# Soft mixture of experts behind attention: W1 multiplied into the rows ahead of the gather, and the gather done 64 columns wide in plain f32

## The chip, the cores and the metric

The kernel runs on one core of one Trainium2 chip. The metric is the time of one execution on the device, in microseconds. The program is one launch with a layer of causal attention and a layer of soft experts, both with their layer norms, on inputs of 2 sequences of 1024 rows of 256 numbers in float32.

## The reference

Attention has 16 heads of 128 (4 groups of keys and values) with rotary embedding; it is not changed. Then, per sequence, with x_ln the normalised rows (1024 x 256), E = 16 experts with S = 128 slots each and H = 64:

```
x_n      = x_ln / max(|x_ln|, 1e-12) * scale          # per row
mu_n     = mu / max(|mu|, 1e-12)                      # per slot
logits   = x_n @ mu_n                                 # n, e, s
dispatch = softmax(logits, over the 1024 rows)        # per slot
combine  = softmax(logits, over all 2048 slots)       # per row
slot_in  = dispatch.T @ x_ln                          # e, s, 256
h        = gelu(slot_in @ W1 + b1)                    # e, s, 64
slot_out = h @ W2 + b2                                # e, s, 256
out      = combine @ slot_out                         # n, 256
```

followed by the sum with the input and a layer norm.

## The kernel before

Each engine has its own queue, and all five walk one list of items (`plan_experts` writes it out); an item is issued on the engine that owns its kind, and waits by semaphores for what it needs. So the order of the list is the order on each engine, and an engine that waits holds up all that is behind it.

There are 32 experts g to go through (16 for each sequence), four to a unit (u = 0 to 7), and a slot s of the list is one step of the loop over them, j = s mod 4. For each expert: `logits` on TensorE (12 matmuls of 512 columns, L1387) into the psum tensor `ring`, of which there is one; `top` on VectorE takes the maximum (L1695, L1697); `exp` on ScalarE (ACT) writes exps (L1568); `keep` on ACT copies the logits out (L1579), after which `ring` is free for the next logits; `run` on VectorE keeps a running maximum (L1708); `inverse` is the reciprocal of the sum (L1720). `turn` transposes exps on TensorE in two halves of 512 columns (L1397) into `turned`, two banks used in turn. Each half is copied out twice: `turned_hi` on ACT rounds it to fp32r (L1508), `turned_lo` on VectorE takes the rest (L1713).

A pair of experts is gathered in the odd slots: `gather` (L1419) multiplies the rows, split in the same way into `row_parts`, with the turned exps: for each of 8 tiles of rows and each half c of the 256 features three matmuls of 256 columns (high by high, high by low, low by high). `gathered` on VectorE multiplies by the reciprocals of the sums (L1736), which `wide_inverse` (L1407) and `inverse_taken` (L1726) have spread over the partitions. When a unit is complete, `hidden` multiplies by W1 (L1431, plain f32), `gelu` on ACT (L1589), `output` multiplies by W2 (L1441), `slot_hi` and `slot_lo` split the result, and `spread` (L1481, eight tiles in four pairs over the next slots) multiplies with the weights of `combine`. `peaks`, `peak`, `fade`, `faded` and `wide`, in slot j = 3, carry the maximum of a row from unit to unit; `shift` on GpSimd (POOL) subtracts it.

The psum tensor `small` has two banks, filled in turn by gather, hidden and output. `free_small` makes a fill wait for the reader of the fill two before it. The rows are split by `rows_hi` (ACT, L1502) and `rows_lo` (VectorE, L1756) once a sequence, in slot 0 and, at the change of sequence, behind logits(16). W1 of a unit is loaded by SP after the `hidden` of the unit before.

The matmuls on fp32r tiles stand as one record each in the profile; plain f32 matmuls as two, transposes as one.

Of the kernel before, what the change touches and what calls it, by code (L numbers as in the profile page):

```python
# [214 lines left out]
def attend(shared, gamma_d, beta_d, row_scale_d, nc, y_sb, slot_vectors, mu_loaded, mu_d, x_d, wq_d, wk_d, wv_d, wo_d, head_scale_d, cos_d, sin_d, ident_d, hidden_d):  # L215
# [51 lines left out]
    with ExitStack() as ctx:  # L267
# [13 lines left out]
        norms, inv_mu, ffn_scale = (shared[name] for name in ("norms", "inv_mu", "scale"))  # L281
# [438 lines left out]
        def _(dve):  # L720
# [18 lines left out]
            for kind, *which in plan:  # L739
# [4 lines left out]
                if kind == "mu_inv":  # L744
                    dve.wait_ge(done["mu_norms"], 1)
                    step(nc.vector.tensor_scalar(norms[:, :], norms[:, :], L2_EPS, None, ALU.max))
                    settle()
                    nc.vector.reciprocal(inv_mu[:, :], norms[:, :]).then_inc(done[kind], 1)
# [28 lines left out]
                if kind == "row_scale":  # L777

                    dve.wait_ge(done["row_length"], 1)
                    dve.wait_ge(row_consts_loaded, 3 * 16)  # L780
                    step(nc.vector.tensor_scalar(row_std[:, :], row_std[:, :], L2_EPS, None, ALU.max))
                    settle()
                    step(nc.vector.reciprocal(row_factor[:, :], row_std[:, :]))
                    settle()
                    nc.vector.tensor_scalar(row_factor[:, :], row_factor[:, :], ffn_scale[:, 0:1], None, ALU.mult).then_inc(done[kind], 1)
# [182 lines left out]
def plan_experts(sequences, experts, tiles):  # L968
# [46 lines left out]
    def split_rows(b):  # L1015
        put(("rows_hi", b, 0), ("rows_hi", b, 1))
# [27 lines left out]
    put(("mu_hi", 0), ("mu_lo", 0), ("mu_hi", 1), ("mu_lo", 1))  # L1044
    put(("logits", 0), ("top", 0), ("exp", 0), ("keep", 0), ("run", 0), ("inverse", 0))
    split_mu(2)

    for s in range(total + 3):
# [6 lines left out]
        if changed:  # L1055
            put(("hidden", v))
            spread(v - 1, (4, 5))
# [3 lines left out]
        if live:  # L1061
            for half in range(2):
                put(("turn", s, half), ("turned_hi", s, half), ("turned_lo", s, half))
# [8 lines left out]
        if ripe and j == 0:  # L1072
            if not changed:
                put(("hidden", v))
# [7 lines left out]
        if s == 0:  # L1082
            split_rows(0)
        if ahead and not change:
            put(("top", s + 1))
        if s == 0:
            put(("rows_lo", 0, 0), ("rows_lo", 0, 1))
# [17 lines left out]
        if j in (1, 3) and live:  # L1105
            put(("gather", s // 2, 0))
# [3 lines left out]
        if j in (1, 3) and live:  # L1110
            put(("gather", s // 2, 1))
# [28 lines left out]
        split_mu(s + 3)  # L1140
        early(s)
# [7 lines left out]
def soft_experts(nc, y_sb, raw_mu, mu_loaded, gamma_d, beta_d, mu_d, scale_d, w1_d, b1_d, w2_d, b2_d, ident_d, out_d):  # L1149
# [4 lines left out]
    with ExitStack() as keep:  # L1154
        def stay(name, shape, dt=F32):
# [4 lines left out]
                  "norms": stay("norms", [P, E]), "inv_mu": stay("inv_mu", [P, E]), "scale": stay("scale", [P, 1])}  # L1160
# [4 lines left out]
def experts(nc, shared, y_sb, raw_mu, mu_loaded, mu_d, w1_d, b1_d, w2_d, b2_d, out_d):  # L1165
# [23 lines left out]
    SMALL = ("gather", "hidden", "output")  # L1189
    TURNED = ("turn", "turn_unit", "peaks", "wide", "wide_inverse")  # L1190
    small_fills = [item for item in plan if item[0] in SMALL and (item[0] != "gather" or item[2] == 0)]
# [3 lines left out]
    with ExitStack() as ctx:  # L1195
# [11 lines left out]
        ident, gamma, beta, scale, inv_mu = (shared[name] for name in ("ident", "gamma", "beta", "scale", "inv_mu"))  # L1207
        rowsT = shared["xT"]
        rows = shared["rows"]
        row_parts = sb("row_parts", [P, 2, TILES, D], F32R)  # L1210
# [5 lines left out]
        dispatch = sb("dispatch", [P, 2, TILES, 2, S], F32R)  # L1216
        exps = sb("exps", [P, N])
        inverse_wide = sb("inverse_wide", [P, 2, S])
        gathered = sb("gathered", [P, KT, UNIT, S])
# [74 lines left out]
        def _(sp):  # L1294
# [16 lines left out]
            for kind, *which in plan:  # L1311
# [5 lines left out]
                if kind == "hidden" and which[0] + 1 < UNITS:  # L1317
                    sp.wait_ge(done["hidden"], which[0] + 1)
# [12 lines left out]
        def _(pe):  # L1331
# [3 lines left out]
            def free_small(item):  # L1335

                n = small_at[item]
                if n >= 2:
# [3 lines left out]
                    if kind == "hidden":  # L1342
                        pe.wait_ge(done["gelu"], count("gelu", *which))
# [4 lines left out]
            def free_turned(item):  # L1348

                n = turned_at[item]  # L1350
                if n >= 2:
                    kind, *which = turned_fills[n - 2]
                    if kind == "turn":
                        pe.wait_ge(done["turned_lo"], count("turned_lo", *which))
# [11 lines left out]
            for item in plan:  # L1366
# [33 lines left out]
                if kind == "wide_inverse":  # L1400
# [8 lines left out]
                    last.then_inc(done[kind], 1)  # L1409
                if kind == "gather":  # L1410

                    pair, c = which
                    if c == 0:
                        pe.wait_ge(done["turned_lo"], count("turned_lo", 2 * pair + 1, 1))
                        pe.wait_ge(done["rows_lo"], count("rows_lo", 2 * pair // E, 1))
                        free_small(item)
# [5 lines left out]
                    last.then_inc(done[kind], 1)  # L1422
                if kind == "hidden":

                    (v,) = which
                    pe.wait_ge(done["gathered"], 2 * v + 2)
                    pe.wait_ge(w1_loaded, (v + 1) * KT * 16)
                    free_small(item)
                    for k in range(UNIT):
# [497 lines left out]
```

## Time and profile before

| | |
|---|---|
| median of 3 executions | 1257.33 us (1255.71 to 1257.91) |
| span of the profiled execution (first to last instruction) | 1253.6 us |
| the profiled execution's own time | not recorded beside its span |
| median less span | 3.7 us |
| TensorE, matmuls | busy 1182.8 us, 94% |
| VectorE | busy 802.1 us, 64% |
| ScalarE | busy 756.3 us, 60% |
| GpSimd | busy 698.0 us, 56% |
| mean granted TensorE clock | 0.982 of full speed |

The busy times overlap, since the engines run beside each other. PE stands for TensorE's matmuls, PEld for its weight loads, DVE for VectorE. The attention part fills the first 845 us, the experts the rest.

### The profile page before, as it was taken

Reading aid. Unit: us, or ns where it says so; the run is one execution under the profiler, and the core shown is the slowest. Engines: PE = TensorE matmul, PEld = TensorE weight load, DVE = VectorE, ACT = ScalarE, POOL = GpSimd, SP = SyncE. Lnnn points to the kernel's source line nnn. Section 1 sums busy time; section 2 is a strip of 40 time slices with the busy share of each in tenths; the row PEclk is TensorE's granted clock in tenths of the full one; section 3 lists DMA queues with packets and bytes.
Section 4 is the critical chain, followed back from the end, with each engine's and each line's share of the span. In section 5 each row is a group of like instructions: output and inputs, shape, how many; then the busy total and the mean of one; then the engine's idle time right before and its main releaser. Section 6 shows DMA issues by size and latency. Waiting matters only on the chain. (4 is left out here: it accounts for less than half of the span.)

```text
span 1253.6 us, 22955 instructions
## 1 busy us (share of the span) xinstructions
PE 1182.8 (94%) x7968; PEld 1084.0 (86%) x7968; DVE 802.1 (64%) x1836; ACT 756.3 (60%) x1442; POOL 698.0 (56%) x473
## 2 busy tenths in 40 slices
PE   4899999999999999999999999997899999989996
PEld 3799998899989998999899889986799988888986
DVE  5565675565665676567656666675566666776666
ACT  2555665656665567667665666544678757556552
POOL 1767767657756674777855765401357535426430
PEclk9999999999999999999999999997999999999999
DMA  2331211121111211121112211101101101011101
GB/s 96 81 106 43 55 31 42 31 56 43 30 26 47 56 26 31 43 56 30 43 31 48 50 26 26 27 1 26 30 14 31 30 9 26 18 27 43 34 10 34
DMA packets 48769, 47.52 MB, mean 38 GB/s; under 512 B 13065, under 2 KB 43273, under 8 KB 48401
## 3 DMA queue, kind: packets, MB, share of 16 engines
q1 hardware_dynamic: 48368, 45.99, 14.3%
q8 instruction: 66, 1.08, 0.4%
q14 instruction: 47, 0.38, 0.1%
q10 hardware_dynamic: 288, 0.07, 0.0%
HBM read 24.03 MB, written 2.10 MB: 21 GB/s over the span
## 5 line engine op out<-in xcount | busy, mean ns | idle before, releaser
L527 PE MATMUL ring<-kT,qT 128*128 128x384 f32 (+5 forms) x1152 | 246.6, 350 | 11.9 <-ACT exps L694 6.4
L829 DVE CUSTOM_DVE_ANT_0 ring<-ring,hidden 128x128 f32<-128x128 f32 (+7 forms) x256 | 190.5, 773 | 91.3 <-PE ring L527 91.0
L694 ACT ACTIVATE exps<-ring,neg_max 128x128 f32<-128x128 f32 (+7 forms) x256 | 189.4, 742 | 68.7 <-DVE neg_max L829 68.6
L527 PEld LDWEIGHTS ring<-kT,qT 128*128 128x128 f32 x1152 | 187.0, 190 | 24.8 <-issue 5.2
L710 ACT ACTIVATE exp_parts<-turned 128x512 fp32r<-128x512 f32 x192 | 114.3, 596 | 139.1 <-PE turned L542 116.5
L565 PE MATMUL mix<-exp_parts,v_parts 128*128 128x256 f32 x1152 | 184.5, 296 | 0.4 <-DVE exp_parts L848 0.4
L542 PE MATMUL turned<-ident,exps 128*128 128x128 f32 x1152 | 179.0, 273 | 1.5 <-DVE exp_parts L848 1.0
L848 DVE TENSOR_TENSOR exp_parts<-turned,exp_parts 128x512 fp32r<-128x512 f32 x192 | 131.8, 686 | 48.2 <-ACT exp_parts L710 47.9
L542 PEld LDWEIGHTS turned<-ident,exps 128*128 128x128 f32 x1152 | 141.8, 141 | 20.0 <-ACT exps L694 1.9
L565 PEld LDWEIGHTS mix<-exp_parts,v_parts 128*128 128x128 f32 x1152 | 149.4, 190 | 0.6 <-DVE exp_parts L848 0.6
L954 POOL TENSOR_TENSOR cos_part<-taken,cos_sb 128x1024 f32<-128x1024 f32 x38 | 91.1, 2396 | 100.5 <-ACT taken L662 100.5
L957 POOL TENSOR_TENSOR rotated<-rotated,sin_sb 128x1024 f32<-128x1024 f32 x38 | 91.1, 2397 | 77.1 <-DMA rotated<-taken 77.1
L835 DVE TENSOR_TENSOR mixed<-mix,mixed 128x256 fp32r<-128x256 f32 x128 | 53.6, 418 | 95.8 <-ACT mixed L717 95.8
L1387 PE MATMUL ffn_ring<-xT,ffn_mu 128*128 128x512 f32 x384 | 106.1, 429 | 2.9 <-POOL ffn_mu L1852 2.5
L577 PE MATMUL ring<-wo_sb,mixed 128*128 128x256 f32 x768 | 105.8, 286 | 1.2 <-DVE mixed L835 0.9
L863 DVE SCALAR_TENSOR_TENSOR y_sb<-ring,inv_sum,y_sb 128x256 f32<-128x256 f32 x256 | 105.7, 475 | 0.5 <-PE ring L577 0.3
L561 PE MATMUL mix<-exps_turned,v_sb 128*128 128x256 f32 (+1 forms) x512 | 105.4, 329 | 0.0
L1419 PE MATMUL ffn_small<-ffn_dispatch,ffn_row_parts 128*128 128x256 f32 x768 | 98.5, 285 | 0.3
L577 PEld LDWEIGHTS ring<-wo_sb,mixed 128*128 128x128 f32 x768 | 96.2, 190 | 2.1 <-DVE mixed L835 1.5
L1419 PEld LDWEIGHTS ffn_small<-ffn_dispatch,ffn_row_parts 128*128 128x128 f32 x768 | 94.1, 189 | 1.0 <-DVE ffn_dispatch L1713 1.0
L1387 PEld LDWEIGHTS ffn_ring<-xT,ffn_mu 128*128 128x128 f32 x384 | 76.0, 205 | 21.5 <-POOL ffn_mu L1852 2.7
L961 POOL TENSOR_TENSOR cos_part<-cos_part,rotated 128x1024 f32<-128x1024 f32 x38 | 91.0, 2396 | 5.5
(205 smaller groups left out, 2112.2 us busy)
## 6 DMA issues: line engine op xcount, KB each, us to landing
rotated<-taken SPq DMA_DIRECT2D x76, 256.0 KB, 3.7
raw_q<-in_L_attn_Wq_dram SPq DMA_DIRECT2D x32, 128.0 KB, 3.6
raw_o<-in_L_attn_Wo_dram SPq DMA_DIRECT2D x32, 128.0 KB, 3.3
ffn_mu_next<-in_L_ffn_mu_dram SPq DMA_DIRECT2D x28, 128.0 KB, 2.5
y_sb<-in_L_attn_x_dram SPq DMA_DIRECT2D x2, 1024.0 KB, 7.5
exps_and_mu<-in_L_ffn_mu_dram SPq DMA_DIRECT2D x1, 2048.0 KB, 9.4
ffn_w_sb<-in_L_ffn_W_dram SPq DMA_DIRECT2D x16, 128.0 KB, 2.4
ffn_w_sb<-in_L_ffn_W_dram SPq DMA_DIRECT2D x8, 256.0 KB
```

Of the source, the lines that this page charges most:

```text
L527: last = nc.tensor.matmul(ring_cols(item, half * BANK, piece), qT[:, H % QUERIES, a, i * P:(i + 1) * P], kT[:, G % 2, m, half * piece:(hal ...
L542: last = nc.tensor.transpose(bank[:, k * P:(k + 1) * P], exps[w][:, i, j * P:(j + 1) * P], ident[:, :])
L561: last = nc.tensor.matmul(out, v_sb[:, G % 2, j * P:(j + 1) * P], exps_turned[:, slot_at[H, w, p] % 2, cols], start=j == 0, stop=alone)
L565: last = nc.tensor.matmul(out, v_parts[:, G % 2, a, j * P:(j + 1) * P], exp_parts[:, slot_at[H, w, p] % HELD, m, cols], start=j == 0 and k ...
L577: last = nc.tensor.matmul(ring_cols(item, t * D, D), mixed[:, window % 2, a, t * P:(t + 1) * P], wo_sb[:, H % 2, m, :], start=k == 0, stop ...
L694: nc.scalar.activation(dst, tile, ACT.Exp, bias=neg_max[:, H % 2, i:i + 1], scale=-1.0, accum_out=row_sum[:, H % 2, i:i + 1]).then_inc(don ...
L710: nc.scalar.activation(exp_parts[:, slot % HELD, 0, :], turned[:, n % 2, :], ACT.Copy).then_inc(done[kind], 1)
L829: nc.vector.tensor_tensor_reduce(tile, tile, later, -1.0, 3.0e38, ALU.add, ALU.min, neg_max[:, H % 2, i:i + 1]).then_inc(done[kind], 1)
L848: nc.vector.tensor_tensor(exp_parts[:, slot % HELD, 1, :], turned[:, n % 2, :], exp_parts[:, slot % HELD, 0, :].bitcast(F32), ALU.subtract ...
L863: last = nc.vector.scalar_tensor_tensor(y_row, ring_cols(("output", H, w), t * D, D), inv_sum[:, H % 2, i:i + 1], y_row, ALU.mult, ALU.add)
L1387: last = nc.tensor.matmul(ring[:, half * BANK:(half + 1) * BANK], mu[:, g % 3, a, c, :], rowsT[:, m, c, half * BANK:(half + 1) * BANK], st ...
L1419: last = nc.tensor.matmul(small_at_item(("gather", pair, 0))[:, c * 2 * S:(c + 1) * 2 * S], row_parts[:, a, t, c * P:(c + 1) * P], dispatc ...
```

## The change

W1 is multiplied into the rows first: `fold` computes rows @ W1 for the four experts of a unit, a matrix of 1024 x 256 in eight tiles, two tiles a fill, and the gather then works on its 64 columns per expert instead of on 256 features. `fold` takes the unit rows already in `rowsT` (split in high and low), times W1 split by `w1_hi` (ACT) and `w1_lo` (POOL); `folded_a` (ACT) and `folded_b` (VectorE) copy the fills out in turn and multiply them by the length of each row (`lengths`), with which the division by the length is taken back. The sign of `scale` is kept with the rows and its size goes into `inv_mu`. The gather is in plain f32; the first expert of the pair goes to output partitions 0 to 63, the second to 64 to 127. `row_parts`, `rows_hi`, `rows_lo`, `hidden` and the low part of `dispatch` are gone, and each half of a turn is copied once, the first by ACT (`turned_a`), the second by VectorE (`turned_b`).

The order of the list:

```diff
+    def take_fold(u, i):
+        put(("folded_b" if i % 2 else "folded_a", u, i))
+
+    def fold(u, fills):
+        if u < units and u % 4:
+            for i in fills:
+                put(("fold", u, i))
+                take_fold(u, i)
+
+    def begin(g):
+        u = g // 4
+        put(("logits", g), *[("fold", u, i) for i in range(4)], ("top", g))
+        take_fold(u, 0)
+        put(("exp", g), ("keep", g), ("run", g), ("inverse", g))
+        for i in range(1, 4):
+            take_fold(u, i)
...
-    put(("logits", 0), ("top", 0), ("exp", 0), ("keep", 0), ("run", 0), ("inverse", 0))
+    begin(0)
...
-            put(("gather", s // 2, 0))
+            put(("gather", s // 2))
         if j == 3 and live:
             put(("wide", u, 0), ("widened_a", u), ("wide", u, 1), ("widened_b", u))
...
-        if j in (1, 3) and live:
-            put(("gather", s // 2, 1))
...
         if ahead and not change:
             put(("run", s + 1), ("inverse", s + 1))
         if j in (1, 3) and live:
             put(("gathered", s // 2))
...
+            fold(u + 1, (0, 1) if j == 1 else (2, 3))
         if change:
-            put(("logits", s + 1))
-            split_rows(1)
-            put(("rows_lo", 1, 0), ("rows_lo", 1, 1))
-            put(*[(kind, s + 1) for kind in ("top", "exp", "keep", "run", "inverse")])
+            begin(s + 1)
...
+        if j == 0:
+            split_w1(u + 1)
```

The new and changed matmuls, and the ring of `small`:

```diff
-    SMALL = ("gather", "hidden", "output")
+    SMALL = ("gather", "fold", "output")
...
                     if kind == "gather":
                         pe.wait_ge(done["gathered"], count("gathered", which[0]))
-                    if kind == "hidden":
-                        pe.wait_ge(done["gelu"], count("gelu", *which))
+                    if kind == "fold":
+                        taken_by = "folded_b" if which[1] % 2 else "folded_a"
+                        pe.wait_ge(done[taken_by], count(taken_by, *which))
...
+                if kind == "fold":
+                    u, i = which
+                    pe.wait_ge(done["w1_lo"], u + 1)
+                    if u == PER:
+                        pe.wait_ge(done["unit_lo"], TILES // 2)
+                    free_small(item)
+                    for half in range(2):
+                        t = 2 * i + half
+                        for n, (c, a, m) in enumerate(passes):
+                            last = nc.tensor.matmul(small_at_item(item)[:, half * UNIT * H:(half + 1) * UNIT * H],
+                                                    rowsT[:, a, c, t * P:(t + 1) * P], w1_parts[:, m, c, :],
+                                                    start=n == 0, stop=n == len(passes) - 1)
+                    last.then_inc(done[kind], 1)
                 if kind == "gather":
-                    pair, c = which
+                    (pair,) = which
+                    u = pair // 2
+                    pe.wait_ge(done["turned_a"], 2 * pair + 2)
+                    pe.wait_ge(done["turned_b"], 2 * pair + 2)
+                    pe.wait_ge(done["folded_a"], count("folded_a", u, 2))
+                    pe.wait_ge(done["folded_b"], count("folded_b", u, 3))
+                    free_small(item)
                     for t in range(TILES):
-                        for k, (a, m) in enumerate(PARTS):
-                            last = nc.tensor.matmul(small_at_item(("gather", pair, 0))[:, c * 2 * S:(c + 1) * 2 * S], row_parts[:, a, t, c * P:(c + 1) * P],
-                                                    dispatch[:, m, t].rearrange("p k s -> p (k s)"),
-                                                    start=t == 0 and k == 0, stop=t == TILES - 1 and k == 2)
+                        for k in range(2):
+                            at_k = 2 * (pair % 2) + k
+                            last = nc.tensor.matmul(small_at_item(item)[k * H:(k + 1) * H, 0:S], folded[:, u % 2, t, at_k * H:(at_k + 1) * H],
+                                                    dispatch[:, t, k, :], start=t == 0, stop=t == TILES - 1)
...
-                    for c in range(KT):
-                        last = nc.vector.tensor_tensor(gathered[:, c, ks, :],
-                                                       small_at_item(("gather", pair, 0))[:, c * 2 * S:(c + 1) * 2 * S].rearrange("p (k s) -> p k s", k=2),
-                                                       inverse_wide[:, :, :], ALU.mult)
+                    for k in range(2):
+                        rows_k = slice(k * H, (k + 1) * H)
+                        last = nc.vector.tensor_tensor(gathered[:, 2 * (pair % 2) + k, :], small_at_item(("gather", pair))[rows_k, 0:S],
+                                                       inverse_wide[rows_k, k, :], ALU.mult)
```

## Rows read from the trace of the kernel before

**Rows 1.** The page, part 1: busy time, share of the span, instructions.
```profile
PE 1182.8 (94%) x7968; PEld 1084.0 (86%) x7968; DVE 802.1 (64%) x1836; ACT 756.3 (60%) x1442; POOL 698.0 (56%) x473
```
**Rows 2.** Chain that ended last, slot 25: start us, us, what.
```profile
1147.00 2.80 PE ffn_ring L1387 x12
...
1150.02 5.75 PE ffn_small L1419 x48
1155.77 0.87 PE ffn_turned L1397 x8
1156.64 2.80 PE ffn_ring L1387 x12
```
**Rows 3.** Timeline, the same slot, DVE and ACT.
```profile
1150.06 0.43 DVE L1726 COPY ffn_inverse_wide<-ffn_turned 128x256 f32<-128x256 f32 x1 [0.21 <-PE ffn_turned L1407]
...
1150.40 1.21 DVE L1695 TENSOR_REDUCE ffn_neg_max<-ffn_ring 128x1 f32<-128x1024 f32 x1
...
1153.23 1.11 ACT L1579 ACTIVATE ffn_kept<-ffn_ring,inv_mu 128x1024 f32<-128x1024 f32 x1
...
1154.37 1.23 DVE L1708 TENSOR_TENSOR ffn_run<-ffn_run,ffn_kept 128x1024 f32<-128x1024 f32 x1 [2.51 <-ACT ffn_kept L1579]
...
1155.52 0.15 DVE L1720 RECIPROCAL ffn_inv_total<-ffn_total 128x1 f32<-128x1 f32 x1
...
1155.81 0.76 DVE L1736 TENSOR_TENSOR ffn_gathered<-ffn_small,ffn_inverse_wide 128x256 f32<-128x256 f32 x2
...
1156.88 0.69 DVE L1713 TENSOR_TENSOR ffn_dispatch<-ffn_turned,ffn_dispatch 128x512 fp32r<-128x512 f32 x1 [0.31 <-ACT ffn_dispatch L1508]
```
**Rows 4.** Chain, slot 27 to 28; then weight loads of L1431 by form.
```profile
1177.02 0.87 PE ffn_turned L1397 x8
1177.89 1.94 PE ffn_small L1431 x16
1179.83 3.00 PE ffn_ring L1387 x12
...
L1431 PEld LDWEIGHTS ffn_small<-ffn_gathered,ffn_w_sb 128*64 128x64 f32 x128 | 13.8, 137 | 2.7 <-DVE ffn_gathered L1736 2.3 <-issue 0.4
```
**Rows 5.** Timeline, slot 27, ACT and DVE.
```profile
1173.08 0.21 ACT L1595 ACTIVATE ffn_fade<-ffn_fade 128x8 f32<-128x8 f32 x1 [6.24 <-DVE ffn_fade L1790]
...
1176.80 0.16 DVE L1720 RECIPROCAL ffn_inv_total<-ffn_total 128x1 f32<-128x1 f32 x1
```
**Rows 6.** Timeline and chain, slot 19: the maximum, and the next logits.
```profile
1075.30 1.22 DVE L1695 TENSOR_REDUCE ffn_neg_max<-ffn_ring 128x1 f32<-128x1024 f32 x1
...
1085.61 2.99 PE ffn_ring L1387 x12
```
**Rows 7.** Timeline, first expert (ACT), and change of sequence (DVE).
```profile
855.49 1.11 ACT L1579 ACTIVATE ffn_kept<-ffn_ring,inv_mu 128x1024 f32<-128x1024 f32 x1
...
1031.33 5.96 DVE L1756 TENSOR_TENSOR ffn_row_parts<-rows,ffn_row_parts 128x1024 fp32r<-128x1024 f32 x2 [0.40 <-ACT ffn_row_parts L1502]
```
**Rows 8.** Windows: length, busy PE, PEld, DVE, ACT, POOL (count), clock, DMA share, GB/s.
```profile
880.00:884.00 4.00, 1.10 (x8) 0.67 (x7) 2.94 (x8) 1.88 (x3) 0.00 (x0) 0.99 0.00 0
884.00:889.00 5.00, 4.93 (x17) 3.65 (x15) 3.71 (x13) 3.78 (x8) 1.47 (x1) 0.66 0.09 26
1037.00:1041.00 4.00, 1.83 (x16) 1.54 (x14) 1.64 (x3) 2.25 (x3) 2.51 (x1) 0.99 0.06 12
1041.00:1046.00 5.00, 4.92 (x18) 3.85 (x17) 2.97 (x7) 4.95 (x10) 0.94 (x1) 0.66 0.01 2
1111.00:1115.00 4.00, 1.38 (x12) 1.18 (x11) 3.46 (x4) 3.08 (x4) 0.00 (x0) 1.00 0.12 33
1115.00:1120.00 5.00, 5.00 (x43) 4.97 (x43) 3.21 (x9) 3.18 (x5) 1.46 (x1) 1.00 0.01 2
```
**Rows 9.** Timeline, last unit: shift released weights, then output.
```profile
1221.06 1.06 ACT L1606 ACTIVATE exps_and_mu<-exps_and_mu 128x1024 f32<-128x1024 f32 x1 [1.18 <-POOL exps_and_mu L1875]
...
1225.33 1.89 PE L1441 MATMUL ffn_small<-ffn_w_sb,ffn_hidden_h 65*128 65x256 f32 x8
```

More of the change, by code:

```diff
@@ L1013, in split_mu, with split_w1 @@
             put(("mu_hi", g), ("mu_lo", g))
-    def split_rows(b):
-        put(("rows_hi", b, 0), ("rows_hi", b, 1))
+    def split_w1(u):
+        if u < units:
+            put(("w1_hi", u), ("w1_lo", u))
+    def take_fold(u, i):
[12 more added lines that the diff above has]
+            take_fold(u, i)
     def turn_units(b, js):
@@ L1062, in plan_experts @@
             for half in range(2):
-                put(("turn", s, half), ("turned_hi", s, half), ("turned_lo", s, half))
+                put(("turn", s, half), ("turned_b" if half else "turned_a", s, half))
         if ripe and j == 1 and not last_unit:
@@ L1187, in count @@
         return at[(kind, *which)] + 1
[L1189 removed]
+    SMALL = ("gather", "fold", "output")
     TURNED = ("turn", "turn_unit", "peaks", "wide", "wide_inverse")
[L1191 removed]
+    small_fills = [item for item in plan if item[0] in SMALL]
     small_at = {item: n for n, item in enumerate(small_fills)}
@@ L1316, in _ @@
                     sp.dma_start(mu_next[:, g % 2], mu_d.rearrange("(c p) e s -> p c e s", p=P)[:, :, g % E, :]).then_inc(done[kind], 16)
-                if kind == "hidden" and which[0] + 1 < UNITS:
-                    sp.wait_ge(done["hidden"], which[0] + 1)
+                if kind == "w1_lo" and which[0] + 1 < UNITS:
+                    sp.wait_ge(done["w1_lo"], which[0] + 1)
                     load_w1(which[0] + 1)
@@ L1423, in _ @@
[L1423 to L1429, printed above, removed]
-                        for c in range(KT):
-                            last = nc.tensor.matmul(small_at_item(item)[0:H, k * S:(k + 1) * S], w1_sb[:, c, k, :],
-                                                    gathered[:, c, k, :], start=c == 0, stop=c == KT - 1)
+                if kind == "fold":
[11 more added lines that the diff above has]
+                    last.then_inc(done[kind], 1)
@@ L1495, in _ @@
                     nc.scalar.activation(mu[:, g % 3, 0], mu_of(g), ACT.Copy).then_inc(done[kind], 1)
-                if kind == "rows_hi":
-                    b, half = which
-                    if b:
-                        act.wait_ge(done["squares"], TILES // 2)
-                        act.wait_ge(done["gather"], E)
-                    ts = slice(4 * half, 4 * half + 4)
-                    nc.scalar.activation(row_parts[:, 0, ts, :], rows[:, ts, :], ACT.Copy).then_inc(done[kind], 1)
-                if kind == "turned_hi":
+                if kind == "w1_hi":
+                    (u,) = which
+                    act.wait_ge(w1_loaded, (u + 1) * KT * 16)
+                    if u:
+                        act.wait_ge(done["fold"], count("fold", u - 1, 3))
+                    nc.scalar.activation(w1_parts[:, 0, :, :], w1_sb[:, :, :, :].rearrange("p c e h -> p c (e h)"), ACT.Copy
+                                         ).then_inc(done[kind], 1)
+                if kind == "folded_a":
+                    u, i = which
+                    act.wait_ge(done["fold"], count("fold", u, i))
+                    if u >= 2:
+                        act.wait_ge(done["gather"], 2 * (u - 1))
+                    for half in range(2):
+                        t = 2 * i + half
+                        last = nc.scalar.activation(folded[:, u % 2, t, :], small_at_item(("fold", u, i))[:, half * UNIT * H:(half + 1) * UNIT * H],
+                                                    ACT.Copy, scale=lengths[:, u // PER, t:t + 1])
+                    last.then_inc(done[kind], 1)
+                if kind == "turned_a":
                     g, half = which
@@ L1582, in _ @@
                     (v,) = which
-                    act.wait_ge(done["hidden"], v + 1)
+                    act.wait_ge(done["gathered"], 2 * v + 2)
                     act.wait_ge(consts_loaded, 16)
@@ L1588, in _ @@
                         e = v % PER * UNIT + k
-                        last = nc.scalar.activation(hidden[0:H, k, :], small_at_item(("hidden", v))[0:H, k * S:(k + 1) * S], ACT.Gelu,
+                        last = nc.scalar.activation(hidden[0:H, k, :], gathered[:, k, :], ACT.Gelu,
                                                     bias=b1_sb[:, e:e + 1])
```

95 lines of the change are left out of this document (53 added, 42 removed).

## The prediction

> **What bounds the kernel now.** I read the shares first, then the stretches by window, then the chain that ended last, and at last the timeline of the engines beside it. TensorE is busy 94% of the span, the next engine, VectorE, 64% [rows 1]. All that the change touches, but for a few eight-element operations, lies behind 845 us, in the experts' part. There the chain in a steady slot (one slot is one expert, g) is TensorE from end to end: logits, turn, gather, turn, logits with no gap [rows 2]. From one start of logits to the next this slot takes 1156.64 - 1147.00 = 9.64 us, and 9.64 us of matmuls stand in it. So TensorE's work is the bound there, and a change that takes work from it could pay. But what the other engines do beside it is one long chain too [rows 3]: top (the maximum) starts 1150.40, then exp, keep starts 1153.23, run 1154.37, the reciprocal ends 1155.67, and `gathered` ends 1156.57. Today nothing on TensorE waits for `gathered` in that slot. That is what I look at below.
>
> **TensorE's work before and after.** A pair's gather is 48 matmuls of 256 columns in 5.75 us, 0.120 each [rows 2]. `hidden` is 8 plain f32 matmuls of 128 columns on 64-wide weights, 16 records in the profile (each stands as two), 1.94 us: 0.121 a record [rows 4]. A unit (four experts) thus pays 2 x 5.75 + 1.94 = 13.4 us, eight times.
> After: a fold fill is 12 matmuls of 256 columns, 12 x 0.120 = 1.44 us, four a unit = 5.76. A pair's gather is 16 plain f32 matmuls of 128 columns on 64-wide weights, 32 records. If the two halves of the array run one after the other this is 32 x 0.121 = 3.87 us; if they run fully at once, half, 1.94. No row shows two halves at once, so these are the bounds. I take 2.0: the two matmuls of a tile share neither weights nor output partitions, so nothing in the program orders one after the other. A unit then costs 5.76 + 2 x 2.0 = 9.8 us, 3.7 less; at the upper bound 13.5, no less than today.
> The Trainium skill ("TensorE: Matmul & The Clock Gate", Part 3, on packing small matmuls) says that matmuls on distinct column groups run concurrently, and gives 2.38 times for three column tiles of 512 columns; by it the gather is near its lower bound. "TensorEngine Tiling (Array Packing)", Key Properties, says against it that a change of tiling mode drains the engine. `hidden`, also 64 wide, starts directly behind a turn today with no gap in the chain [rows 4], so if it is such a change, the drain is too short to see; by that rule I add nothing.
>
> **The new wait, which decides.** The psum ring `small` has two banks, and a fill waits for the reader of the fill two before it. Its order becomes gather(pair), fold, fold, gather, fold, fold. So the second fold behind each gather waits for `gathered`(pair), and on VectorE `gathered` stands behind run(s+1), hence behind logits, top, exp and keep of the next expert. Behind the waiting fold on TensorE stand turn(s+1) and logits(s+2), the very loop that sets the pace.
> Odd slot, j=1, with folds (s = 1, 5, 9, 17, 21, 25): `gathered` starts behind the reciprocal, 1155.7 [rows 3]. Its two operations shrink to 64 x 128; they can't take more than today's 0.76 for both, nor less than half; 0.5. It ends 1156.3. TensorE gets through gather and first fold by 1150.02 + 2.0 + 1.44 = 1153.5 (1155.3 with the halves in turn), and waits either way. Fold 1156.45 to 1157.9, turn 0.87 to 1158.8, logits 1158.8 instead of 1156.64: +2.1. Slots 5, 17 and 21, where slots' copies are still before top, I put at +2.5. Six slots: 3 x 2.1 + 3 x 2.5 = +13.8.
> Slot j=3 with folds, units with a fade (s = 7, 11, 23, 27): exp waits for ACT's fade, which waits for VectorE's peaks; the reciprocal ends 1176.96 [rows 5]. `gathered` to 1177.5, last fold 1177.65 to 1179.1, turn to 1180.0; logits start 1180.0, today 1179.83 after `hidden` [rows 4]: +0.1. Where today `gathered` waits for the gather (s = 7, 11) it is about -0.5. Sum of four: -0.7.
> Slot j=3 without a fade (s = 3, 19): s = 19 has top at 1075.30 and logits at 1085.61 [rows 6]. Top starts 0.6 earlier, since VectorE copies one half instead of subtracting both (one 128x512 operation is 0.69 [rows 3]). From top to the end of `gathered` it is 5.9 us as in slot 25 [rows 3]: 1080.6, with peaks between 1081.1; fold, turn: logits 1083.5, -2.1. Two slots: -4.2.
> Units 3 and 7 have no folds behind their gathers. In s = 13 and 29 logits could start at the end of keep instead of after 5.75 of gather, but ACT and VectorE's splits of the weights (weight_hi, weight_lo) come next: -0.5 and -1.1.
>
> **The ends.** Start: four folds now stand between logits(0) and turn(0). The fourth waits for folded_b, on VectorE behind top, run and reciprocal, and folded_a (two copies of 256, 0.8) stands ahead of exp. Keep ends 856.60 today [rows 7]; after 857.3, run's copy 0.69 and reciprocal to 858.1, folded_b 0.8 to 858.9, fold 1.44, turn 0.87: logits(1) starts 861.3 instead of 856.7. Today it runs slowly behind its wait [rows 8]; part comes back: +3.5 (2 to 4.6).
> Change of sequence: the 5.96 us of rows_lo between logits(16) and top, which ends at 1037.2 [rows 7], goes, `hidden` too, but the same four folds with the same wait come: fold four ends near 1036.2, then two spreads 2.9 and turn 0.9, logits(17) starts 1040.0 for 1041.3: -2 with the shorter gather and turn before it (-3 to +1).
> End: gelu no longer follows `hidden` but still POOL's shifts; these start 2 us earlier as the gather is shorter. Output starts 2.9 earlier, yet behind 4.9 us of idle: -2 (-3 to 0) [rows 9].
> ACT and VectorE: each loses one 128x512 operation per expert and gains two of 256 per two folds, about even; both have idle time beside TensorE [rows 1]. POOL's w1_lo and the sign operations of the attention part (each some 0.2 us under TensorE's work) I cost at nothing; uncovered they would be 1 us a unit.
> Sum: 13.8 - 0.7 - 4.2 - 1.6 + 3.5 - 2 - 2 = +6.8 us.
>
> **The clock.** The windows give pairs of stretches [rows 8]. In 880 to 884 TensorE was idle for 4.00 - 1.10 = 2.9 us, and in the next five the granted clock was 0.66 (part of the time at the lower of its two levels, 1.2 GHz for 2.4): 4.93 busy us cost 0.34 x 4.93 = 1.7 us. In 1037 to 1041 it was idle 2.2 us, then 0.66 again; in 1111 to 1115 2.6 us, then still 1.00. My j=1 waits are 1156.45 - 1153.5 = 3.0 us, the four j=3 waits with a fade about 2.5. I let the clock fall in four of six of the first and one or two of four of the second: 5.5 x 1.7 = +9.4. If the halves run in turn the waits are 1.1 and 0.6 and it doesn't fall.
> Forecast: 6.8 + 9.4 = +16.2 on the profiled span of 1253.6, 1269.8. From this span to the median of 1257.33 there are 3.7 us (the profiled execution has no time of its own here); I leave them as they are. 1273.5, so 1274.
>
> **Rivals.**
> A, halves in turn: for it, no row of this kernel has them at once. The fold slots keep their length, since `gathered` ends them; the change of sequence, s = 3, 19 and the end lose 3.5 us. 6.8 + 3.5, no clock loss: 1267.6. 23%.
> B, halves at once, clock stays up: for it the 2.6 us of 1114; against it the two others. 1264. 18%.
> C, faster: TensorE's shorter work shows and the wait does not. It decides where `gathered` ends before the first fold does, 1153.5, that is, 2.8 us earlier than I say. Then j=1 slots have 0.9 less and j=3 slots 2.6 less, and with the ends the sum is 6 x -0.9 + 6 x -2.6 - 1.6 - 0.5 = -23: 1234. Against it stands the written order and rows 3, in which logits' end to run's end has hardly a gap. 8%.
> D, the 64-wide weight loads, 0.137 each [rows 4], aren't hidden: a gather of 32 x 0.18 = 5.8 us. Then first folds end behind `gathered`, +0.7 in j=1 and +1.2 in j=3 on A, six each: 1279. 8%.
> The forecast itself has 38%, its own range 1268 to 1281; 5% is left for small terms that cancel the sum.
>
> **How the numbers follow.** The range runs from 1259 (B with the three ends at their better bounds, 3.5 us, and 2 us less in the slots) to 1284 (the forecast with the clock falling in all ten long waits, 1281, and 3 us of waits that I didn't see). Less than 0.2% (2.5 us) is about what a measurement can't tell from no change: 7%. Faster by more: C and 3 of the rest, 11%. No change: the other 2 and 5 of B's. Slower: 82%.
>
> **What would show it.** Right: idle time on TensorE before the new fold matmuls, released by VectorE's `gathered`, in twelve slots, some 2 to 3 us each; unit length about 46 us instead of 44; gather 32 records in about 2 us; 0.6 to 0.7 clock behind some waits. 3.9 us for the gather would be A. Wrong: folds that follow each other without a wait, or logits to logits below 10 us in a j=1 slot with folds.

## The result, and the profile after

The changed kernel takes 1277.33 us (median; 1272.01 to 1278.24), the kernel before 1257.03 in the same series: 1.0156 times as long, 95% interval 1.0135 to 1.0176. It is slower by 20 us; the forecast was 1274. The profiled execution took 1278.24, its span is 1276.3 and its mean granted clock 0.971, beside 1253.6 and 0.982 before.

The page after, part 1, answers to [rows 1]. TensorE is busy for 16 us less, and the kernel is longer (the busy time holds what the lower clock adds; by the prediction's sum of 3.7 us a unit the work itself is some 30 us less):

```profile
PE 1166.7 (91%) x7968; PEld 1065.9 (84%) x7968; DVE 790.7 (62%) x1838; ACT 754.1 (59%) x1446; POOL 704.4 (55%) x481
```

Timeline of TensorE after (start us, us, engine, line; in brackets the idle time ahead of it and what released it): the start, slot 1, the end of slot 5's fills, the change of sequence, slot 25 and slot 27.

```profile
857.15 4.57 PE L1444 MATMUL ffn_small<-ffn_w_parts,xT 128*128 128x256 f32 x36 [1.01 <-POOL ffn_w_parts L1901]
863.78 1.72 PE L1444 MATMUL ffn_small<-ffn_w_parts,xT 128*128 128x256 f32 x12 [2.06 <-DVE ffn_folded L1763]
...
884.34 1.78 PE L1444 MATMUL ffn_small<-ffn_w_parts,xT 128*128 128x256 f32 x12 [2.76 <-DVE ffn_gathered L1788]
885.92 1.91 PE L1421 MATMUL ffn_turned<-ident,ffn_exps 128*128 128x128 f32 x8
887.48 3.78 PE L1411 MATMUL ffn_ring<-xT,ffn_mu 128*128 128x512 f32 x12
...
927.46 2.90 PE L1444 MATMUL ffn_small<-ffn_w_parts,xT 128*128 128x256 f32 x12 [4.01 <-DVE ffn_gathered L1788]
...
1053.51 2.90 PE L1444 MATMUL ffn_small<-ffn_w_parts,xT 128*128 128x256 f32 x12 [2.49 <-DVE ffn_folded L1763]
...
1171.22 1.97 PE L1460 MATMUL ffn_small<-ffn_dispatch,ffn_folded 128*64 128x128 f32 x32
1173.12 1.69 PE L1444 MATMUL ffn_small<-ffn_w_parts,xT 128*128 128x256 f32 x12
1177.58 1.67 PE L1444 MATMUL ffn_small<-ffn_w_parts,xT 128*128 128x256 f32 x12 [2.77 <-DVE ffn_gathered L1788]
1179.09 1.03 PE L1421 MATMUL ffn_turned<-ident,ffn_exps 128*128 128x128 f32 x8
1179.88 3.01 PE L1411 MATMUL ffn_ring<-xT,ffn_mu 128*128 128x512 f32 x12
...
1200.90 1.67 PE L1444 MATMUL ffn_small<-ffn_w_parts,xT 128*128 128x256 f32 x12 [2.54 <-DVE ffn_gathered L1788]
```

In slot 25 the reader sees what replaced [rows 2]. The gather takes 1.97 us instead of 5.75, the first fold follows at once, and the second stands 2.77 us idle. Its clock did not fall. Behind the wait of slot 1 the same turn takes 1.91 us and the same logits 3.78, where slot 25 has 1.03 and 3.01: there it did. Whether it falls changes from execution to execution. In e10, the same kernel once more, it fell in slot 25 too, behind the same wait:

```profile
1174.58 2.90 PE L1444 MATMUL ffn_small<-ffn_w_parts,xT 128*128 128x256 f32 x12 [2.76 <-DVE ffn_gathered L1788]
```

The chain that ended last, in slot 25 (start us, us, what), is no longer TensorE's from end to end:

```profile
1168.33 2.75 PE ffn_ring L1411 x12
...
1171.67 1.23 DVE ffn_neg_max L1735
...
1174.50 1.12 ACT ffn_kept L1618
...
1176.95 0.18 DVE ffn_gathered L1788
...
1177.58 1.67 PE ffn_small L1444 x12
1179.25 0.87 PE ffn_turned L1421 x8
```

That is [rows 3] once more, maximum, exp, keep, run, reciprocal and `gathered`, but now TensorE waits for its last link. The four largest of TensorE's waits in the experts' part, by releaser (us in total, times, longest):

```profile
PE ffn_small L1444 <- DVE ffn_gathered L1788: 31.4, 12, 4.0
PE ffn_turned L1421 <- ACT ffn_exps L1607: 9.3, 5, 2.9
PE ffn_small L1470 <- ACT ffn_hidden_h L1628: 5.1, 1, 5.1
PE ffn_small L1444 <- DVE ffn_folded L1763: 4.5, 2, 2.5
```

Windows behind such waits (length, busy PE, PEld, DVE, ACT, POOL, clock, DMA share, GB/s) answer to [rows 8]: in this trace the clock falls in slots 1, 5 and 17, and not in slot 25.

```profile
884.00:888.00 4.00, 3.66 (x21) 3.65 (x22) 1.21 (x4) 0.60 (x1) 0.22 (x1) 0.72 0.11 33
928.00:933.00 5.00, 5.00 (x23) 4.81 (x22) 1.73 (x4) 1.55 (x2) 1.67 (x2) 0.50 0.09 26
1078.00:1083.00 5.00, 4.50 (x21) 4.53 (x22) 1.22 (x4) 1.22 (x4) 2.71 (x2) 0.50 0.10 30
1178.00:1182.00 4.00, 4.00 (x28) 3.65 (x27) 2.26 (x4) 1.55 (x2) 1.80 (x2) 1.00 0.11 33
```

**Where the time is.** From each start of logits to the next, in both traces and in those of the experiments, summed by kind of slot (j=1: slots 1, 5, 9, 17, 21, 25; j=3: slots 3, 7, 11, 19, 23, 27; begin: the first two starts; change: slots 14 to 16; "first" is the start of the first logits, "end" what follows the last; us):

```
kernel                      first   begin  j=1    j=3    change  others  end    span
before                      847.1   18.7   62.3   86.2   44.6    141.7   53.0   1253.6
changed                     851.5   23.3   82.4   83.6   43.9    137.3   54.3   1276.3
e1 gathered first           850.7   23.5   59.7   69.2   43.8    148.9   54.9   1250.7
e3 halves in turn           849.6   23.1   76.9   83.8   47.1    136.0   56.6   1273.1
e5 e1 + order in begin()    848.9   19.6   58.5   69.3   39.8    148.7   54.6   1239.3
e6 all                      844.9   19.0   59.2   69.8   39.8    147.5   47.8   1228.1
e7 e1 + halves in turn      850.2   23.1   66.7   76.0   47.0    144.7   55.9   1263.5
e8 first fold twice         848.9   22.8   78.5   80.6   44.0    136.8   54.5   1266.1
e9 before, gathered first   847.2   18.4   60.9   87.0   46.0    152.4   54.1   1266.0
e10 changed again           849.8   23.5   85.3   86.6   42.5    135.8   54.3   1277.7
```

Of the 22.7 us between the two spans, 20.1 stand in the six j=1 slots, 4.6 at the beginning and 4.4 ahead of the experts' part; the rest gives 6.4 back. The two traces of the changed kernel differ by 5.9 us in the twelve slots with folds (166.0 and 171.9), since the clock falls behind more waits in the second.

**Those 4.4 us** lie in the attention part, where the new sign operations are. Timeline after (POOL's and VectorE's operations near 361 us, then TensorE):

```profile
360.50 2.39 POOL L965 TENSOR_TENSOR rotated<-rotated,sin_sb 128x1024 f32<-128x1024 f32 x1 [1.99 <-DMA rotated<-taken]
361.11 1.82 DVE L747 TENSOR_SCALAR norms<-norms 128x16 f32<-128x16 f32 x1
...
363.04 2.35 POOL L969 TENSOR_TENSOR cos_part<-cos_part,rotated 128x1024 f32<-128x1024 f32 x1
...
363.33 2.08 DVE L753 TENSOR_TENSOR scale<-scale,sign 128x1 f32<-128x1 f32 x1
...
365.91 0.68 DVE L856 TENSOR_TENSOR exp_parts<-turned,exp_parts 128x512 fp32r<-128x512 f32 x1
...
366.73 0.92 PE L542 MATMUL turned<-ident,exps 128*128 128x128 f32 x4 [2.78 <-DVE exp_parts L856]
```

A product of one element per partition takes 2.08 us and ends when POOL's operation, begun 0.3 us ahead of it, ends. TensorE waits 2.78 us for the exp_parts behind it. The kernel before has these rows in VectorE's timeline, with exp_parts 3.3 us earlier:

```profile
360.46 1.93 DVE L746 TENSOR_SCALAR norms<-norms 128x16 f32<-128x16 f32 x1
...
362.59 0.63 DVE L848 TENSOR_TENSOR exp_parts<-turned,exp_parts 128x512 fp32r<-128x512 f32 x1
```

The first logits start at 848.9 to 851.5 in the traces that have these operations in this place (seven in the table), at 847.1 and 847.2 in the two without; so of the 4.4 us some 3 are the operations' and the rest is scatter.

### The profile page after: what moved, and what is told of

The parts are those of the page before. It is cut to its first block and busy times, and to the rows that moved or that the text cites. A ratio compares the mean times of both kernels' runs of the same rounds, so it can differ in the third digit from the quotient of the medians.

```text
span 1276.3 us, 23033 instructions
## 1 busy us (share of the span) xinstructions
PE 1166.7 (91%) x7968; PEld 1065.9 (84%) x7968; DVE 790.7 (62%) x1838; ACT 754.1 (59%) x1446; POOL 704.4 (55%) x481
## 5 line engine op out<-in xcount | busy, mean ns | idle before, releaser
L1411 PE MATMUL ffn_ring<-xT,ffn_mu 128*128 128x512 f32 x384 | 102.5, 418 | 3.2 <-POOL ffn_mu L1897 2.5
L969 POOL TENSOR_TENSOR cos_part<-cos_part,rotated 128x1024 f32<-128x1024 f32 x38 | 91.0, 2394 | 5.5
L1444 PE MATMUL ffn_small<-ffn_w_parts,xT 128*128 128x256 f32 x384 | 59.8, 313 | 36.9 <-DVE ffn_gathered L1788 31.4
L561 PEld LDWEIGHTS mix<-exps_turned,v_sb 128*128 128x128 f32 x512 | 87.8, 192 | 6.7
L1411 PEld LDWEIGHTS ffn_ring<-xT,ffn_mu 128*128 128x128 f32 x384 | 74.9, 202 | 19.6 <-POOL ffn_mu L1897 3.0
```

The source lines that it names most:

```text
L561: last = nc.tensor.matmul(out, v_sb[:, G % 2, j * P:(j + 1) * P], exps_turned[:, slot_at[H, w, p] % 2, cols], start=j == 0, stop=alone)
L1411: last = nc.tensor.matmul(ring[:, half * BANK:(half + 1) * BANK], mu[:, g % 3, a, c, :], rowsT[:, m, c, half * BANK:(half + 1) * BANK], st ...
L1444: last = nc.tensor.matmul(small_at_item(item)[:, half * UNIT * H:(half + 1) * UNIT * H], rowsT[:, a, c, t * P:(t + 1) * P], w1_parts[:, m, ...
```

## The experiments

### e1: `gathered` ahead of `run`

```diff
+        if j in (1, 3) and live:
+            put(("gathered", s // 2))
         if ahead and not change:
             put(("run", s + 1), ("inverse", s + 1))
         if j in (1, 3) and live:
-            put(("gathered", s // 2))
```

> `gathered` of a pair is issued by VectorE ahead of `run` and `inverse` of the next expert; nothing else changes. Theory (the second fold waits for `gathered`, which stands behind run): VectorE reaches `gathered` about when logits' maximum is taken, before the first fold ends, so the waits of 2 to 4 us before the second folds go, the clock no longer falls behind them, j=1 slots with folds take about 8.8 us (9.3 in slots 5, 17, 21) instead of 11.4 to 14.5, j=3 slots 2 us less. Time 1277 - 26 (six j=1 slots) - 12 (six j=3 slots) - 2 = about 1237. Rival 1 (the time is in the added copies of ACT and VectorE, which lengthen the chain from top to run): waits only move, 1270 to 1277. Rival 2 (only the clock costs): the slots lose the slow part alone, 1277 - 9 = 1268.

Measured: 1249.35 us (1247.51 to 1252.6), 0.9953 of before (0.9937 to 0.9969): 28 us less than the changed kernel, by the place of one item (27, when each is set against the kernel before of its own series). Timeline of TensorE and VectorE's `gathered` in slot 25:

```profile
1147.19 2.99 PE L1412 MATMUL ffn_ring<-xT,ffn_mu 128*128 128x512 f32 x12
...
1150.33 1.97 PE L1461 MATMUL ffn_small<-ffn_dispatch,ffn_folded 128*64 128x128 f32 x32
1152.23 3.14 PE L1445 MATMUL ffn_small<-ffn_w_parts,xT 128*128 128x256 f32 x24
...
1152.34 0.59 DVE L1789 TENSOR_TENSOR ffn_gathered<-ffn_small,ffn_inverse_wide 64x128 f32<-64x128 f32 x2
...
1155.99 3.01 PE L1412 MATMUL ffn_ring<-xT,ffn_mu 128*128 128x512 f32 x12
```

Both folds run in one piece of 24 matmuls, and the slot takes 8.80 us (9.64 before, 11.80 changed). The theory stands and both rivals fall. But 1237 was expected. The twelve fold slots gave 37.1 of the 38 us hoped for in them; the other slots got 11.6 longer. TensorE's waits say for what:

```profile
PE ffn_ring L1412 <- POOL ffn_mu L1898: 4.8, 2, 2.5
...
PE ffn_spread L1511 <- DVE ffn_weights L1820: 3.8, 3, 2.9
PE ffn_spread L1511 <- DVE ffn_mixed L1849: 3.6, 1, 3.6
```

In the changed kernel these were 2.5, 0.5 and 1.7 us. The slots that got longest are 22 and 24 (14.0 and 16.5 us, 9.4 and 13.1 in the changed kernel). A faster TensorE meets the parts of mu on POOL and, on VectorE, the splits of the weights and the sums of `spread`. VectorE itself got slower at the same work: its 30 run operations behind the first two take 45.4 us in e1 and 37.9 in the changed kernel, and each that takes over 1.5 us, for the usual 1.23, runs beside an operation of POOL. That these are the whole of the 11.6 us was not tried.

### e2 and e4: the sign operations left out, and moved

e2 leaves out the sign operations and |scale| in inv_mu (scale is 1 in these inputs, and the sign is set to 1). e4 computes all, five steps later:

```diff
-        if H == 12 and n == 3:
+        if H == 12 and n == 8:
             plan.append(("mu_inv",))
```

> Leaves out the multiplication of inv_mu by |scale| in the attention part (scale is 1 in these inputs): the sign and scale operations of VectorE near 361 us go, the experts' part stays as in the changed kernel. Theory (a VectorE operation of 128x1 that starts while POOL runs its tensor operation of 2.35 us ends only with it, and the exp_parts behind it make TensorE wait): the offset of 3.7 us at 366 us goes, 1277.3 - 3.7 = 1273.6. Rival (the offset is noise between executions, or something else in the attention part): 1277, and the experts' part starts at 851.5 as before.

> The changed kernel with the four sign and scale operations, and the two of inv_mu beside them, issued five steps later in the attention part (near 372 us instead of 361), where POOL's tensor operations leave a gap; the computation is whole. Theory (what cost 3.7 us were VectorE operations that stood still beside POOL's operation of 2.35 us, not their number): TensorE's wait of 2.78 us at 366.7 us goes, the experts' part starts near 847.3 as in the kernel without these operations, 1277.3 - 4 = 1273. Rival (the operations and their waits for each other cost it wherever they stand): 851.5 and 1277.

Measured: e2 1272.49 us (1266.74 to 1276.44), first logits at 846.8; e4 1269.63 (1268.93 to 1274.41), 1.0119 of before (1.0098 to 1.0141), first logits at 843.5. The rival of e4 falls: the same operations cost nothing elsewhere. Timeline of VectorE in e4, 0.4 us after POOL's operation of 366.87 + 2.40 us has ended:

```profile
369.67 0.17 DVE L747 TENSOR_SCALAR norms<-norms 128x16 f32<-128x16 f32 x1
...
370.24 0.16 DVE L753 TENSOR_TENSOR scale<-scale,sign 128x1 f32<-128x1 f32 x1
```

The product takes 0.16 us instead of 2.08, and norms 0.17 instead of 1.82, now that POOL is idle. Norms stood still in the kernel before too, and in e2 (1.82 us); I read e4's 7.7 us against e2's 4.8 as the norms' share, and with it that e4 came out below the 1273 expected; no run moves norms alone. The clock and the scatter of these runs leave a us or two of it open.
The Trainium skill ("SBUF — State Buffer", Who interferes with whom) says that VectorE and GpSimd share a pair of ports by an exclusive lock, taken by a VectorE instruction with two SBUF inputs beside a GpSimd one that reads SBUF; the later one blocks until the first is done. By that rule L753 would stand still until L969 ends, and the trace agrees: 363.33 + 2.08 = 365.41, against 363.04 + 2.35 = 365.39.

### e3 and e7: the two column halves one after the other

The same edit on the changed kernel (e3) and on e1 (e7):

```diff
-                    for t in range(TILES):
-                        for k in range(2):
+                    for k in range(2):
+                        for t in range(TILES):
```

> The gather's loop over the two experts is put outside the loop over the tiles, so that its 16 matmuls of one column half run before the 16 records of the other start. Theory (the halves run at once only because matmuls for the two halves alternate; the end of `gathered`, not TensorE's work, ends the fold slots): gather 3.9 us instead of 1.97, waits before the second folds shrink by 1.9 to 1 to 2 us, the clock no longer falls behind them; fold slots get shorter by the clock's share, 6 to 9 us, the change of sequence, slots 3 and 19, units 3 and 7 and the end get 3 to 5 us longer: 1271 to 1274. Rival 1 (the gather's length counts on TensorE's path): 1277 + 16 x 1.9 = 1307. Rival 2 (the array overlaps them in either order): gather stays 1.97 us and the time 1277.

> The kernel with `gathered` ahead of `run`, and the gather's two column halves one after the other (3.33 us instead of 1.97). Theory (without the wait TensorE's own work ends the slots, so now the gather's length counts, which it did not with the wait in place): 12 to 16 gathers x 1.36 = 16 to 22 us more, 1249.4 + 19 = 1268. Rival (another engine's chain bounds now, and the concurrency of the halves is worth nothing): 1249 to 1254.

Measured: e3 1276.75 us (1275.06 to 1279.4), e7 1264.52 (1263.34 to 1265.43), 1.0067 of before (1.0044 to 1.0089). The gather in slot 25 of e3, and the second fold behind it, by the timeline of TensorE:

```profile
1165.77 3.33 PE L1460 MATMUL ffn_small<-ffn_dispatch,ffn_folded 128*64 128x128 f32 x32
...
1172.13 1.67 PE L1444 MATMUL ffn_small<-ffn_w_parts,xT 128*128 128x256 f32 x12 [1.41 <-DVE ffn_gathered L1788]
```

The gather has 3.33 us instead of 1.97, the wait 1.41 instead of 2.77, and the second fold starts as long after the gather's start as before (6.36 us both times). Sixteen gathers longer by 1.36, 21.8 us of TensorE's time, leave the total where it was; rival 1 (1307) falls. My own 1271 to 1274 was too low: the j=1 slots gave back 5.5 us, and the change of sequence and the end cost 5.5. In e7, where nobody waits for `gathered`, the same edit costs 15.2 us, a little less than the 16 to 22 expected; the rival (no cost) falls. So the concurrency of the halves is worth 15 us, and in the changed kernel nothing.

### e5: the order in begin()

```diff
-        put(("exp", g), ("keep", g), ("run", g), ("inverse", g))
-        for i in range(1, 4):
+        put(("exp", g))
+        take_fold(u, 1)
+        put(("keep", g), ("run", g), ("inverse", g))
+        for i in (2, 3):
             take_fold(u, i)
```

> The kernel with `gathered` ahead of `run`, and in begin() VectorE's copy of the second fold put directly behind `top`, ahead of run and inverse. Theory (the fourth fold at the start and at the change of sequence waits for this copy behind run): the two waits of 2.1 and 2.4 us go, the first slot takes about 12.5 us instead of 15.7, the one at the change about 13.5 instead of 16.2; 1249.4 - 6 = 1243.5. Rival (the chain top, exp, keep, run ends these slots anyway, with an added copy of 0.9 us ahead of run): 1249 to 1250.

Measured: 1241.18 us (1241.05 to 1241.3), 0.9884 of before (0.9866 to 0.9902), 8.2 us less than e1. The first slot takes 12.04 us for 15.71, the one at the change 12.23 for 16.24, and the waits for `folded` of 2 us and more are gone from TensorE's list. That is 2.3 us better than the 1243.5 expected. The rival falls.

### e8: the first fold twice

```diff
-                    for half in range(2):
+                    for half in [h for h in range(2) for _ in range(2 if u % PER and i % 2 == 0 else 1)]:
```

> The changed kernel, in which each first fold behind a gather is computed twice into the same bank (12 more matmuls, 1.44 us at the full clock, twelve times; the result is the same). Theory (the wait's end is set by `gathered`, and the clock falls because TensorE stands idle in it): the added 17 us of work lie in the waits and cost nothing but 0.3 us in slots 3 and 19, the waits shrink to 1.3 to 2.5 us and the clock falls in fewer slots, so the time is that of the changed kernel or less: 1268 to 1277, 1271 most likely. Rival (TensorE's work is on the path): 1277 + 12 x 1.44 = 1294.

Measured: 1267.88 us (1266.58 to 1268.2), 1.0095 of before (1.0075 to 1.0114). With 17 us of needless matmuls the kernel is 9.5 us faster (8.7, each against the kernel before of its own series), at the lower edge of what was expected. Between the two traces 2.7 us stand ahead of the first logits, which these matmuls can't touch, and 6.9 in the fold slots (12.8 against e10's trace). The timeline of TensorE in slot 17, first in the changed kernel, then in e8:

```profile
1078.50 2.90 PE L1444 MATMUL ffn_small<-ffn_w_parts,xT 128*128 128x256 f32 x12 [3.51 <-DVE ffn_gathered L1788]
...
1066.48 3.13 PE L1444 MATMUL ffn_small<-ffn_w_parts,xT 128*128 128x256 f32 x24
1071.68 1.67 PE L1444 MATMUL ffn_small<-ffn_w_parts,xT 128*128 128x256 f32 x12 [2.07 <-DVE ffn_gathered L1788]
1073.19 1.04 PE L1421 MATMUL ffn_turned<-ident,ffn_exps 128*128 128x128 f32 x8
```

The wait is 2.07 us instead of 3.51, fold and turn take 1.67 and 1.04 instead of 2.90 and 1.91, and the slot 12.56 instead of 14.51. So the clock's share is shown by itself: it is what idle TensorE costs behind its wait. In slots 5 and 9, where 2.57 and 2.43 us of the wait are left, the clock still falls:

```profile
922.00:927.00 5.00, 4.33 (x22) 4.26 (x23) 1.75 (x6) 1.90 (x5) 2.88 (x2) 0.66 0.09 26
971.00:976.00 5.00, 5.00 (x25) 4.80 (x26) 1.61 (x4) 1.55 (x2) 2.11 (x2) 0.66 0.09 26
```

### e9: the same order in the kernel before

The diff has the same effect as e1's, on the kernel before.

> The kernel before, with only `gathered` ahead of `run`. Theory (there no fill of TensorE waits for `gathered` in a steady slot, and the gather ends 1.4 us behind the start of run, so the new order delays run by some 2 us and takes nothing off TensorE's path): same or slower, 1256 to 1266. Rival (the order alone is worth the 28 us that it took from the changed kernel): 1230.

Measured: 1269.3 us (1268.57 to 1269.76), 1.0102 of before (1.0086 to 1.0117): slower, and by more than the 1266 that was expected at most. The rival falls. TensorE waits there for what comes after run, and run itself takes longer (the last line: VectorE's operation, its count, us in total and mean ns):

```profile
PE ffn_spread L1484 <- DVE ffn_weights L1777: 8.9, 6, 3.7
PE ffn_turned L1410 <- DVE ffn_dispatch L1716: 5.7, 6, 1.5
...
L1711 DVE TENSOR_TENSOR ffn_run<-ffn_run,exps_and_mu 128x1024 f32<-128x1024 f32 x16 | 30.3, 1894 | 7.2 <-ACT exps_and_mu L1582 7.2
```

These waits were 2.6 and 4.1 us before. The order that is right with a gather of 2 us is wrong with one of 5.75: ahead of 15 of the 16 `gathered` VectorE stands idle for 2.2 to 4.0 us until the gather is done. Run comes later by that, and falls beside POOL's operations: a mean of 1894 ns in the line above for 1223 in the kernel before, and 53.5 us in sum for 37.4. How the 13 us divide between the later start and the longer run was not tried.

### e6 and e10: all together, and the changed kernel again

e6 is e5 with e4's move and, at the last unit, gelu ahead of two weights on ACT:

```diff
+            put(("gelu", v))
             if last_unit:
                 put(("weight", v, 1), ("weight", v, 0))
-            put(("gelu", v))
```

> `gathered` ahead of `run`, the order in begin(), the sign operations five steps later, and at the last unit gelu ahead of the two weights on ACT (the output waited 5.1 us for gelu). Theory: the parts add up, 1241.2 (the first two) - 4 (sign) - 2 (gelu, two operations of 1.05 us earlier) = 1235. Rival (what TensorE gains at one place it waits for at the next, as three slots got 2 to 5 us longer when `gathered` went ahead of run): 1239 to 1241.

> The changed kernel once more beside them, unchanged, so that its time and its profile stand on the same chip: 1272 to 1278, and 12 waits for `gathered` of some 31 us in sum. If the clock falls behind other waits than in the first profile, single slots differ by up to 2 us.

Measured: e6 1231.61 us (1230.0 to 1233.74), 0.9802 of before (0.9788 to 0.9815). e10 1277.89 us (1271.64 to 1280.97), 1.0158 (1.0131 to 1.0185), with 31.3 us of waits for `gathered` in twelve slots. e6's forecast was 1235: the parts add up, and the end gave more than the 2 us expected: it is 47.8 us instead of 54.6. Timeline of e6 at the output:

```profile
1199.41 1.99 PE L1473 MATMUL ffn_small<-ffn_w_sb,ffn_hidden_h 65*128 65x256 f32 x8 [1.05 <-ACT ffn_hidden_h L1631]
```

and in the changed kernel:

```profile
1245.24 3.78 PE L1470 MATMUL ffn_small<-ffn_w_sb,ffn_hidden_h 65*128 65x256 f32 x8 [5.14 <-ACT ffn_hidden_h L1628]
```

4.1 us of wait and 1.8 of slow clock behind it are gone.

The computation of the change, in an order that fits it, is 25 us faster than the kernel before and 46 us faster than the changed kernel. A part of the 25 is not the change's: moving norms would help the kernel before too (not tried).

## Why the prediction was right

**The wait that decides: right.** It stands in all twelve slots named, released by `gathered`, 1.1 to 4.0 us each and 31.4 us in sum; in slot 25 the second fold starts 9.25 us after logits, where 9.45 was worked out from [rows 3] (1156.45 - 1147.00). A unit got 3.7 us longer (48.6 for 44.9, the mean over slots 4 to 11 and 20 to 27), where the sign named was 2. e1 shows the wait to be the cause.

**The halves: right.** 32 records in 1.97 us, 62 ns each, against 104 with the halves in turn (e3) and 121 in `hidden` [rows 4]. A, the rival of halves in turn, fell by that row; its reason why the length would not count (`gathered` ends the slots) was right as well, as e3 shows. D fell: no weight load lengthens the gather (its 0.18 us a record stood in no row).

**j=1 slots:** forecast +13.8, and 4 falls of the clock at 1.7 us, +20.6; measured +20.1. Single slots differ: slot 1 only +1.0, since before it had its own slow clock; slots 5, 9, 17 and 21 +3.7 to +4.8, with the clock down behind the wait; slot 25, where it stays up, +2.2 for the +2.1 worked out.
**j=3 slots:** -4.9 and 1.5 falls, -2.3; measured -2.6; slots 3 and 19 -4.1 for the -4.2 forecast from [rows 6], the four with a fade [rows 5] +1.5, two of them with a slow clock.
**The clock:** it fell where the forecast put it, behind these waits; B, the clock staying up, falls by the windows at 928 and 1078, and e8 gives back 6.9 us without taking all waits away. How often it falls was a guess: 5.5 times in the sum, behind seven of the ten waits of 2 us and more in the first trace, behind all ten in e10. In e10 the j=1 slots are +23.0 and the j=3 slots +0.4, so that +20.1 and -2.6 came within half a us of the forecast is in part luck.

**Mis-sized:** the beginning +4.6 for +3.5 [rows 7] (the wait for POOL's w1_lo, 1.01 us, was put at nothing); the change of sequence -0.7 for -2; the other slots -4.4 for -1.6 (slots 13 and 29, which have no folds, gave 1.9 and 2.0 us, not 0.5 and 1.1); the end +1.3 for -2. Its output does start earlier, 23.3 us after the last logits for 24.8 before, but behind 5.1 us of idle it and the spread that follows run at the lower clock, 3.78 and 4.34 us for 1.89 [rows 9] and 3.23, and that takes more than the gain back; the clock at the end was no term of the sum. Together these four come to +2.9 us.

**Wrong:** the sign operations at nothing. "each some 0.2 us under TensorE's work" took a duration from an undisturbed row; the kernel before already had norms at 1.93 us beside POOL, next to the place of the new ones. By e2 the term is 3 to 5 us (the starts of the first logits, the medians).

**Luck in the total:** on the span the forecast was 1269.8 and the first trace has 1276.3, 6.5 us more: 4.4 ahead of the first logits and 2.9 mis-sized, less 0.8 in the fold slots. The 3.7 us from span to median, carried over from the kernel before, are 1.0 in the changed kernel, and that hid 2.7 of it. So the median is only 3.3 us above 1274; the mechanism was right, and the closeness of the total owes something to this.

**C, the faster case,** was priced at 1234 if `gathered` came early. e1 makes it come early: 1249. C's gain in the twelve fold slots was 21.0 us and e1 has 19.6; but the other slots got 7.2 us longer than before, where C had them 1.6 shorter, and the beginning 4.8 longer.

## What to carry to other kernels

When an operation becomes shorter, look at who reads its buffer and where that reader stands in its own queue: a two-bank ring binds the second fill behind it to that place. Here one item's place in VectorE's list was worth 28 us, about as much as the whole saving of matmuls (some 30 us by the prediction's 3.7 a unit), and the same move made the old kernel 13 us slower; so set the order again after the work changes. A wait on TensorE costs more than its length where the clock falls behind it, and that can differ between two executions of one kernel. And cost a small VectorE operation by what runs on GpSimd beside it, not by its size.

## What the runs showed of the hardware

- Plain f32 matmuls of 128 columns on 64-wide weights, alternating between the two column halves: 62 ns a record; one half after the other: 104 ns. So two at once are worth 1.69 times, not 2. The Trainium skill ("TensorE: Matmul & The Clock Gate", Part 3, Measured speedup vs the span model) gives a measured 2.38 times for three column tiles of 512 columns; these rows, with two tiles and 128 columns, agree with it in that the gain stays below the number of tiles.
- Added work on TensorE made the kernel faster: 144 matmuls more (e8), 9.5 us less by the medians; between the two traces the slots where they stand took 6.9 us less.
- A VectorE operation on one element per partition took 2.08 us beside POOL's of 2.35, and 0.16 alone. VectorE's run of 128x1024, 1.23 us as a rule, took up to 3.2 us in e9 beside POOL's operations.
- The same wait in the same kernel (2.77 and 2.76 us, slot 25) was followed by full clock in one execution and by half in another (fold 1.67 and 2.90 us).
